# A graph network's layer-4 rows, made in another stage, and three blocks of small VectorE work in another

## The chip, the cores and the metric

The kernel runs on one core of one Trainium2 chip. The core has five engines that run side by side: TensorE (PE in the profile), VectorE (DVE), ScalarE (ACT), GpSimd (POOL) and SyncE (SP), and 16 DMA engines. They wait for each other through semaphores. The metric is the device time in microseconds: 2548.24 us before the change, the median of 3 runs (2527.15 to 2566.37).

## The reference, cut to what matters

Four graph layers on 50,000 nodes with 128 values each and 25,000 edges, sorted by destination. Each layer adds its result to `x` and normalizes the rows.

```python
x = _layernorm(x + _L0_gnn_ref(...))   # layer 1: two attention convolutions, 4 heads x 16, then 1 x 128
x = _layernorm(x + _L1_gnn_ref(...))   # layer 2: mean over the incoming edges
x = _layernorm(x + _L2_gnn_ref(...))   # layer 3: two-layer MLP per edge, then mean, max and sum
x = _layernorm(x + _L3_gnn_ref(...))   # layer 4: attention with both ends of the edge

def gat_layer(x, W, attn_l, attn_r, bias, src, dst, num_nodes):
    feat = (x @ W).reshape(num_nodes, H, D)
    e = jax.nn.leaky_relu(el[src] + er[dst], NEG_SLOPE)
    alpha = ee / s[dst]                                   # softmax over the edges of one destination
    return jax.ops.segment_sum(feat[src] * alpha[:, :, None], dst, num_segments=num_nodes) + bias
```

A node that is the destination of no edge (an isolated node) gets only biases and normalizations in every layer. Its row before layer 4 is therefore a scaled copy of its input row plus a combination of a few fixed bias rows, and the factors of that combination (the rates) follow from the mean, the variance and four dot products of the input row. An edge whose source is such a node needs this row in layer 4: these are the layer-4 rows of isolated sources. They are made for all edges, and a later index picks the ones that are wanted.

## The kernel before

The edges are handled in 49 groups (`NG`) of 512, as 4 tiles of 128 (`GT`). Every engine has its own program, and the whole is a sequence of stages with a barrier after each: a (gathers of the source and destination rows), b (the attention of layer 1's first convolution), c (the lookup stage), d (the projection of layer 1's second convolution), e, f, g and h for the other layers. In each stage the loops run over the 49 groups, and the order of each engine's program is the order of the code. There is no scheduler. `need(engine, name, n)` makes an engine wait until a semaphore has counted n groups; `S(name)` is that semaphore.

Stage b, about 597 to 757 us. For each group VectorE weighs the rows (L1129), TensorE turns them (L1211), VectorE sums over edges with a scan (L1148), ACT takes two Relus and an Exp (L1238 to L1242), VectorE joins them (L1199), TensorE multiplies (L1221), ACT copies to SBUF (L1250). `pipeline` runs these stages with lags and calls the blocks of its list `between` at evenly spaced steps. With two blocks they come at steps 24 and 48 of 51. VectorE's two are the first layer of the edge rates (`rates_vector`, L1064 to L1087) and `map_table`, which makes the table from which stage c looks up nodes. A layer of rates needs one square root from ACT (`rates_scalar`, L1103). Before `map_table` TensorE makes prefix sums (`prefix`, L1227).

Stage c, about 757 to 1045 us. The purpose is to find for each source the row of its first convolution, and to gather it. SP loads for each group the source numbers, copied to all partitions (`slb`, L1457), and the source rows from `xsrc_e` (L1460). VectorE compares the numbers (`hot`, L1345), TensorE looks up 4 tiles in `table` with eight matmuls (L1301, L1302), VectorE picks one value out of each row of the result (L1351), adds a bias to the source rows (`shifted`, L1368, into `z`), and writes four columns of indices (`hid`, L1358, L1361). GpSimd gathers with them four times 128 rows (L658). ACT normalizes the source rows (`apply`, L720), SP stores them (L1465), and ACT copies what was gathered one group before (`copy`, L1427, L1428). VectorE's order in group g is `hot(g+1)`, `pick(g)`, `shifted(g)`, `hid(g)`. SP's order is `load(g)`, `store(g-2)`. Between the groups VectorE has eight larger blocks (the table `extra`): after group 3 `rows_of_biases`, which makes the bias rows `DB`, after 5 and 7 the second and third layer of the edge rates, after 9, 11, 13, 15 and 16 the same for nodes. `QC` is 0, so the code for node rows in this stage (`node`, `rows`, `node_load`) does nothing.

Stage d, about 1067 to 1285 us. VectorE weighs and scans (L1133, L1148), TensorE turns (L1211) and multiplies (L1570), VectorE adds the residual and takes mean and variance (L1554, L674, L683), ACT normalizes (L720). Beside this the layer-4 rows are made: SP loads the source rows again (L1533), TensorE transposes the factors of the group (L1497), ACT copies them (L1516), TensorE adds the rows and the biases in PSUM (L1506 for the rows by the unit matrix, L1507 for factors times `DB`), ACT scales them in four ACTIVATEs (L1524), SP stores them (L1538).

## Time and profile before

| | us |
|---|---|
| median of 3 runs | 2548.24 |
| lowest and highest run | 2527.15, 2566.37 |
| profiled execution, its time | 2542.37 |
| its span, first to last instruction | 2540.6 |
| mean granted clock of TensorE | 0.679 of full speed |

The page of the profile gives busy time for each engine. Over the whole span TensorE is busy 1895.0 us (75%), VectorE 1740.2 (68%), GpSimd 1383.0 (54%), ScalarE 1083.8 (43%). These are sums over stages with different limits, so they must be read by stage. In the views, "idle before" is how long an engine stood before an instruction, and the arrow names what ended that. A granted clock of 1.0 is 2.4 GHz, one of 0.5 is 1.2 GHz. In a mean over a stretch anything between can stand.

### The profile page before, as it was taken

The numbers are of one execution on the slowest core, as the hardware profiler recorded it, in microseconds if no ns is written. First come the engines' busy times: TensorE is split into PE (matmuls) and PEld (weight loads), VectorE is DVE, ScalarE is ACT, GpSimd is POOL, SyncE is SP. The second block draws the span as 40 slices with busy tenths as digits, with TensorE's granted clock in tenths as the row PEclk, the third lists the DMA queues.
The fourth block names the chain that finished last, engine by engine and source line by source line (L and its number), as shares of the span: only waits on it lengthen the run. The fifth ranks groups of instructions, "written<-read, shape, count | busy, mean of one in ns | idle before, by whom it ended". The sixth has DMA issues, their size and how long they took to land.

```text
span 2540.6 us, 30997 instructions
## 1 busy us (share of the span) xinstructions
PE 1895.0 (75%) x7398; PEld 1202.8 (47%) x7398; DVE 1740.2 (68%) x6542; ACT 1083.8 (43%) x3008; POOL 1383.0 (54%) x1388
## 2 busy tenths in 40 slices
PE   3999999867874445399944454999998699959983
PEld 2898888855651112155534342444444122225542
DVE  6444445458769966598768885888887366678773
ACT  0222222215753343287633332666665455524332
POOL 4777777720006577200057771566666677727776
PEclk9656656655556665599756856999999555556565
DMA  4555555553334455288645554333332699933341
GB/s 154 160 155 157 155 152 160 159 188 133 125 127 125 112 156 160 72 278 262 211 131 155 154 159 120 98 112 111 109 106 82 237 363 326 313 105 100 122 135 37
DMA packets 255479, 398.63 MB, mean 157 GB/s; under 512 B 80999, under 2 KB 97536, under 8 KB 255172
## 3 DMA queue, kind: packets, MB, share of 16 engines
q1 hardware_dynamic: 204340, 307.86, 37.2%
q0 software_dynamic: 43904, 75.95, 11.0%
q10 hardware_dynamic: 7056, 12.85, 1.4%
q8 instruction: 62, 1.02, 0.2%
q14 instruction: 117, 0.96, 0.1%
HBM read 225.25 MB, written 178.97 MB: 159 GB/s over the span
## 4 chain that ended last, share of the span: by engine, by line
POOL 17%; issue 12%; PE 9%; DVE 9%; ACT 7%; DMA 3%; SPq 1%; POOLq 0%; DVEq 0%; ACTq 0%
POOL ring L658 9%; POOL big L658 4%; POOL out_dram L664 4%; ACT outr L720 3%; DVE big L1870 2%; ACT big L1809 2%; PE bank L1570 2%; DVE stats L674 2%; PE bank L1507 2%; PE bank L1506 2%; DMA ring<-x_t,idx 1%; PE bank L1211 1%; DVE z L1886 1%; DMA hT<-xsrc_e 1%; DVE mv L683 1%
## 5 line engine op out<-in xcount | busy, mean ns | idle before, releaser
L720 ACT ACTIVATE outr<-z,rn 128x128 f32<-128x128 f32 x784 | 322.7, 483 | 347.9 <-DVE rn L709 155.7
L658 POOL DMA_INDIRECT ring<-in_x_dram,idx x392 | 380.0, 969 | 147.3 <-issue 119.3
L658 POOL DMA_INDIRECT ring<-x_t,idx x280 | 269.0, 961 | 339.6 <-SPq L302 245.3
L658 POOL DMA_INDIRECT ring<-hidden_e,idx x196 | 193.3, 986 | 298.9 <-DVE idx L1361 241.6
L664 POOL DMA_INDIRECT x_t<-outr,idx x196 | 234.6, 1197 | 208.4 <-ACT outr L720 162.0
L1148 DVE TENSOR_TENSOR_SCAN G<-cont,G,bank 64x512 f32<-64x512 uint8 (+1 forms) x192 | 242.8, 1265 | 80.0 <-PE bank L1211 57.2
L664 POOL DMA_INDIRECT out_dram<-outr,idx x196 | 195.2, 996 | 102.7 <-issue 58.2
L1947 PE MATMUL bank<-DB,z 20*128 20x512 f32 x196 | 201.7, 1131 | 22.8 <-DVE xT L1337 7.0
L1020 DVE BATCH_NORM_STATS2 stats<-ring 128x6 f32<-128x128 f32 x196 | 42.8, 281 | 247.9 <-DMA ring<-in_x_dram,idx 247.9
L1301 PE MATMUL bank<-table,hT 128*128 128x391 bf16 x196 | 94.3, 481 | 153.4 <-DVE hT L1345 153.4
L674 DVE BATCH_NORM_STATS2 stats<-z 128x6 f32<-128x128 f32 x784 | 171.0, 281 | 5.1
L1211 PE MATMUL bank<-ident,msg 128*64 128x128 f32 (+1 forms) x588 | 136.3, 377 | 35.1 <-DVE msg L1133 32.2
L1570 PEld LDWEIGHTS bank<-W_s,G 65*128 65x128 f32 (+1 forms) x784 | 130.4, 252 | 65.4 <-issue 64.1
L1647 PE MATMUL bank<-ident,ring 128*128 128x128 f32 x196 | 47.8, 389 | 138.6 <-DMA ring<-x_t,idx 138.6
L1570 PE MATMUL bank<-W_s,G 65*128 65x128 f32 (+1 forms) x784 | 147.6, 348 | 0.0
L938 PEld LDWEIGHTS bank<-bT,msg 128*128 128x128 f32 x784 | 146.1, 277 | 1.0 <-ACT msg L977 0.9
L938 PE MATMUL bank<-bT,msg 128*128 128x4 f32 x784 | 143.5, 306 | 0.7 <-ACT msg L977 0.7
L977 ACT ACTIVATE msg<-bank 128x512 f32<-128x512 f32 x98 | 58.6, 598 | 188.8 <-PE bank L928 188.8
L1917 DVE CUSTOM_DVE_ANT_0 msg<-ring,attb 128x128 f32<-128x128 f32 x280 | 63.9, 288 | 101.9 <-DMA ring<-x_t,idx 59.3
L1211 PEld LDWEIGHTS bank<-ident,msg 128*64 128x64 f32 (+1 forms) x588 | 82.1, 163 | 93.1 <-issue 43.9
L658 POOL DMA_INDIRECT big<-x_t,idx x112 | 107.1, 956 | 34.2 <-issue 34.2
L716 ACT ACTIVATE sd<-mv,epsc 128x4 f32<-128x4 f32 x196 | 56.3, 287 | 157.8 <-DVE mv L683 157.8
(385 smaller groups left out, 4516.7 us busy)
## 6 DMA issues: line engine op xcount, KB each, us to landing
hT<-in_x_dram SPq DMA_DIRECT2D x194, 256.0 KB
ring<-x_e SPq DMA_DIRECT2D x147, 256.0 KB, 2.9
x_t<-outr SPq DMA_DIRECT2D x98, 256.0 KB, 2.7
x_e<-outr SPq DMA_DIRECT2D x98, 256.0 KB, 2.1
x_t<-xload SPq DMA_DIRECT2D x48, 512.0 KB, 3.1
xsrc_e<-ring SPq DMA_DIRECT2D x49, 256.0 KB, 2.1
xd_e<-ring ACTq DMA_DIRECT2D x49, 256.0 KB, 2.9
ring<-xsrc_e SPq DMA_DIRECT2D x49, 256.0 KB
```

The costliest lines, as they stand in the source:

```text
L658: nc.gpsimd.indirect_dma_start(to(c), None, table, bass.IndirectOffsetOnAxis(ap=idx[:, kind, (g + 1) * GT + c:(g + 1) * GT + c + 1].bitcas ...
L664: nc.gpsimd.indirect_dma_start(table, bass.IndirectOffsetOnAxis(ap=idx[:, kind, (g + 1) * GT + c:(g + 1) * GT + c + 1].bitcast(U32), axis= ...
L674: ins = v.bn_stats(stats[:, k, :], z[:, s, k, :])
L720: ins = nc.scalar.activation(to[:, k, :], frm[:, k, :], ACT.Identity, bias=sc[:, k, 1:2], scale=sc[:, k, 0:1])
L938: ins = nc.tensor.matmul(bank[4 + g % 2][:, at:at + 4], dxT[:, h, k * P:(k + 1) * P], bT[:], start=True, stop=True)
L977: nc.scalar.activation(dxT[:, q % 2, :], bank[0][:], ACT.Copy).then_inc(S("n_dxT"), 1)
L1148: return v.tensor_tensor_scan(o, m, src_ap, ini, ALU.mult, ALU.add)
L1211: ins = nc.tensor.transpose(bank[s][0:width, c * P:(c + 1) * P], msg[:, s, c, 0:width], ident[:])
L1301: nc.tensor.matmul(o, lhs, table[:, 0, :], start=True, stop=False)
L1570: ins = nc.tensor.matmul(bank[2 + s][:, c * F:(c + 1) * F], G[0:k, s, c * P:(c + 1) * P], W[:], start=not b, stop=not b or c == GT - 1)
L1917: c.do(v.tensor_tensor_reduce(msg[:, n, k, :], frm, attb[:, n, :], 1.0, 0.0, ALU.mult, ALU.add, dots[:, k, n:n + 1]))
L1947: nc.tensor.matmul(bank[2 + q % 4][:], ecT[q % 4], DB[0:GT * CN, :, :].rearrange("p t f -> p (t f)"), start=True, stop=True).then_inc(S("o ...
```

## The change

The layer-4 rows of isolated sources are made in stage c and no longer in stage d. They use the source rows that stage c has in SBUF anyway (`rload`), so the second load from `xsrc_e` is gone. The matmuls, the ACTIVATEs and the store are the same. In stage c TensorE has them after the lookups of the next group, ACT between the copy of the gathers and the normalization, SP after the store of the layer-1 rows. The lookups use five PSUM banks and no longer six.

For this the rates of all edges must be there before stage c. So the second and third layer of the edge rates and `rows_of_biases` go to stage b, whose list has now five blocks, at steps 12, 20, 28, 36 and 48: first layer, `map_table`, second layer, `rows_of_biases`, third layer. The code for node rows in stage c, which did nothing, is gone too.

```diff
@@ -1190,6 +1190,20 @@
                 c.hold()
             return step
 
+        def rows_of_biases(v):
+            ch = Chain(v)
+
+            def step():
+                for t in range(GT):
+                    for k, n in ((0, 1), (1, 2), (2, 3), (3, None), (4, 0)):
+                        row = ones[0:32, :] if n is None else biasc[0:32, n, :]
+                        at = ident[0:32, CN * t + k:CN * t + k + 1]
+                        if k == 0:
+                            ch.link(v.tensor_scalar(DB[:, t, :], row, at, None, ALU.mult))
+                        else:
+                            ch.link(v.scalar_tensor_tensor(DB[:, t, :], row, at, DB[:, t, :], ALU.mult, ALU.add))
+            return step
...
+            edge = rates_vector(v, 3, "e", ecov, est, alpha3, est, etemps)
             pipeline(v, [(-1, weighing(v, "b", feat, HF, HEADS)), (2, join), (0, scanning(v, "b", HF))],
-                     [rates_vector(v, 3, "e", ecov, est, alpha3, est, etemps)[0], map_table(v)])
+                     [edge[0], map_table(v), edge[1], rows_of_biases(v), edge[2]])
...
-            pipeline(pe, [(0, turning(pe, "b", HF)), (2, project)], [skip, prefix])
+            pipeline(pe, [(0, turning(pe, "b", HF)), (2, project)], [prefix, skip, skip, skip, skip])
...
+            root = rates_scalar(a, 3, "e", etemps)
+            pipeline(a, [(0, split), (2, rows)], [root[0], skip, root[1], skip, root[2]])
...
+        sx = xTf[:, 0:2 * GE].rearrange("p (s e) -> p s e", s=2)
+
+        def local_tensor(pe):
+            def factors(g):
+                need(pe, "s_ecT", g)
+                nc.tensor.transpose(bank[6][0:GT * CN, 0:P], ecov[:, four(g), :].rearrange("p t k -> p (t k)"),
+                                    ident[:]).then_inc(S("s_tr"), 1)
+
+            def local(g):
+                s = g % 2
+                wait(pe, f"c_ld{g % RING}", 16 * (g // RING + 1))
+                need(pe, "s_ecT", g + 1)
+                need(pe, "s_row", g - 1)
+                nc.tensor.matmul(bank[5 + 2 * s][:], ident[:], rload[:, g % RING].rearrange("p t f -> p (t f)"), start=True, stop=False)
+                nc.tensor.matmul(bank[5 + 2 * s][:], hcT[g % 4], DB[0:GT * CN, :, :].rearrange("p t f -> p (t f)"),
+                                 start=False, stop=True).then_inc(S("s_mm"), 1)
+            return factors, local
+        def local_scalar(a):
+            def factors(g):
+                need(a, "s_tr", g + 1)
+                need(a, "s_mm", g - 3)
+                nc.scalar.activation(hcT[g % 4], bank[6][0:GT * CN, 0:P], ACT.Copy).then_inc(S("s_ecT"), 1)
+
+            def local(g):
+                need(a, "s_mm", g + 1)
+                if g >= 2:
+                    wait(a, f"s_out{g % 2}", 16 * (g // 2))
+                for k in range(GT):
+                    ins = nc.scalar.activation(sx[:, g % 2, k * F:(k + 1) * F], bank[5 + 2 * (g % 2)][:, k * F:(k + 1) * F],
+                                               ACT.Copy, scale=alpha3[:, GT * g + k:GT * g + k + 1])
+                ins.then_inc(S("s_row"), 1)
+            return factors, local
+
+        def local_store(sp, g):
+            need(sp, "s_row", g + 1)
+            sp.dma_start(edge_row(x3s_e, g), sx[:, g % 2, :]).then_inc(S(f"s_out{g % 2}"), 16)
...
-                    need(pe, "look_pick", t - 5)
-                    o = bank[t % 6][:, 0:HI]
+                    need(pe, "look_pick", t - 4)
+                    o = bank[t % 5][:, 0:HI]
...
+            factors, local = local_tensor(pe)
             for g in range(NG):
                 look(g)
+                factors(g)
+                if g:
+                    local(g - 1)
+            local(NG - 1)
...
-            edge = rates_vector(v, 3, "e", ecov, est, alpha3, est, etemps)
...
-            extra = {3: rows_of_biases, 5: edge[1], 7: edge[2], 9: node[0], 11: node[1], 13: node[2], 15: node[3],
-                     16: scaled}
+            extra = {9: node[0], 11: node[1], 13: node[2], 15: node[3], 16: scaled}
...
-            root = rates_scalar(a, 3, "e", etemps)
...
+            factors, local = local_scalar(a)
             for g in range(NG + 1):
                 if g in extra:
                     extra[g]()
                 if g < NG:
+                    factors(g)
+                if g:
+                    local(g - 1)
+                if g < NG:
                     apply(g)
...
                 need(sp, "c_z", g - 3)
+                need(sp, "s_mm", g - 3)
                 sp.dma_start(rload[:, g % RING].rearrange("p t f -> p (t f)"), edge_row(xsrc_e, g)) \
                     .then_inc(S(f"c_ld{g % RING}"), 16)
...
                 if g >= 2:
                     store(g - 2)
...
+                    local_store(sp, g - 2)
...
-            if tag == "d":
-                factors, local = local_tensor(pe)
-                pipeline(pe, [(0, turning(pe, tag, width)), (0, factors), (1, project), (1, local)])
-            else:
-                pipeline(pe, [(0, turning(pe, tag, width)), (1, project)])
+            pipeline(pe, [(0, turning(pe, tag, width)), (1, project)])
...
-            linear_sync(sp, "d", xd_e, x1_e, False, "_z", also=local_sync(sp))
-            for s in range(2):
-                sp.wait_ge(S(f"s_out{s}"), 16 * len(range(s, NG, 2)))
+            linear_sync(sp, "d", xd_e, x1_e, False, "_z")
```

What this does to the order of instructions is seen at three places. The first is SP's program at the start of stage c, before the change. `hT<-srclo_d` are the source numbers, `ring<-xsrc_e` the source rows, `x_t<-outr` the store of the layer-1 rows.

```order
L1457 DMA hT<-srclo_d 128x512
L1460 DMA ring<-xsrc_e 128x512
L1465 DMA x_t<-outr 128x512 [waits g_row]
L1457 DMA hT<-srclo_d 128x512 [waits look_oh]
L1460 DMA ring<-xsrc_e 128x512 [waits g_z]
```

The same place with the change. `x_t<-xT` is the store of the layer-4 rows.

```order
L1475 DMA hT<-srclo_d 128x512
L1479 DMA ring<-xsrc_e 128x512
L1484 DMA x_t<-outr 128x512 [waits g_row]
L1345 DMA x_t<-xT 128x512 [waits s_row]
L1475 DMA hT<-srclo_d 128x512 [waits look_oh]
L1479 DMA ring<-xsrc_e 128x512 [waits s_mm,g_z]
```

Before each load of source numbers there stands now a store that waits for `s_row`, which ACT counts up after the four ACTIVATEs of the layer-4 rows.

The second place is ACT's program in stage c, one group, before the change: `big<-ring` is the copy of the gathers, `outr<-z,est` the normalization.

```order
L1427 ACTIVATE big<-ring 128x4x64 [waits g_in0]
L1428 ACTIVATE big<-ring 128x4
L720 ACTIVATE outr<-z,est 128x128 [waits g_out2,g_z]
L720 ACTIVATE outr<-z,est 128x128 x3
L1427 ACTIVATE big<-ring 128x4x64 [waits g_in1]
```

And with the change. `g_in` is the landing of the gathers.

```order
L1451 ACTIVATE big<-ring 128x4x64 [waits g_in1]
L1452 ACTIVATE big<-ring 128x4
L1331 ACTIVATE hT<-bank 20x128 [waits s_mm,s_tr]
L1338 ACTIVATE xT<-bank,dlo 128x128 [waits s_out0,s_mm]
L1338 ACTIVATE xT<-bank,dlo 128x128 x3
L720 ACTIVATE outr<-z,est 128x128 [waits g_out3,g_z]
L720 ACTIVATE outr<-z,est 128x128 x3
```

The factors (L1331) and the layer-4 rows (L1338) stand now directly behind the copy of the gathers, and before the next normalization.

The third place is VectorE's program in stage b with the change, around step 28. The block of the second layer (L1064 to L1089) stands between a scan (L1148) and the next weighing (L1129); before the change no block stood there.

```order
L1213 SCALAR_TENSOR_TENSOR hT<-hT 64x512 [waits b_exp,g_mm]
L1148 SCALAR_TENSOR_TENSOR G<-cont,G,bank 64x512 [waits b_exp,g_scan,g_tr]
L1064 SCALAR_TENSOR_TENSOR cv<-ecov,cv 128x196
L1065 TENSOR_SCALAR cv<-cv,BB 128x196 [waits dve_chain]
L1067 RECIPROCAL cv<-cv 128x196 [waits e_root]
L1069 SCALAR_TENSOR_TENSOR ecov<-ecov,BB,cv 128x196 [waits dve_chain]
L1072 TENSOR_TENSOR cv<-cv 128x196
L1073 TENSOR_TENSOR cv<-cv 128x196 [waits dve_chain]
L1083 TENSOR_TENSOR dlo<-dlo,cv 128x196
L1089 TENSOR_TENSOR ecov<-ecov,cv 128x196 [waits dve_chain]
L1129 TENSOR_TENSOR msg<-big,alpha 128x4x64 [waits g_tr,dve_chain]
```

On ACT the square roots of these layers (`e_root`) come with a load of the activation table before them, and another before the next Exp: there are six table loads in stage b now, and there were two.

## Rows read from the trace of the kernel before

**Rows 1.** Stretches b, c, d: PE, PEld, DVE, ACT, POOL busy; clock, DMA share, GB/s

```profile
597.00:757.00 160.00, 140.73 (x577) 112.14 (x576) 113.93 (x167) 106.65 (x242) 0.00 (x0) 0.51 0.32 123
757.00:1045.00 288.00, 121.53 (x392) 46.78 (x392) 212.40 (x658) 106.09 (x301) 193.28 (x196) 0.62 0.49 135
1067.00:1285.00 218.00, 206.52 (x833) 110.90 (x833) 177.24 (x638) 148.39 (x491) 0.00 (x0) 0.85 0.75 237
```

**Rows 2.** Groups by line, stage c: GpSimd's gathers, busy, mean ns, idle before

```profile
L658 POOL DMA_INDIRECT ring<-hidden_e,idx x196 | 193.3, 986 | 298.9 <-DVE idx L1361 241.6 <-issue 55.2 <-ACT big L1428 2.1
```

**Rows 3.** Timeline, stage c: start us, length us, engine, line, idle before

```profile
949.17 1.46 POOL L658 DMA_INDIRECT ring<-hidden_e,idx  x1 [0.30 <-issue]
...
954.69 0.94 POOL L658 DMA_INDIRECT ring<-hidden_e,idx  x1 [0.30 <-issue]
...
958.23 0.42 ACT L1427 ACTIVATE big<-ring 128x256 f32<-128x256 f32 x1 [5.85 <-DMA ring<-hidden_e,idx]
...
960.67 0.43 SPq L1457 DMA_DIRECT2D hT<-srclo_d  x1
...
960.91 0.42 ACT L1427 ACTIVATE big<-ring 128x256 f32<-128x256 f32 x1 [0.62 <-DMA ring<-hidden_e,idx]
...
963.35 0.57 SPq L1457 DMA_DIRECT2D hT<-srclo_d  x1
...
964.29 0.35 DVE L1345 TENSOR_SCALAR hT<-hT,pcol 128x512 bf16<-128x512 bf16 x1 [3.40 <-DMA hT<-srclo_d]
...
967.58 0.16 DVE L1361 SCALAR_TENSOR_TENSOR idx<-hidt,dhi 128x4 int32<-128x4 f32 x1
...
967.91 0.43 DVE L1345 TENSOR_SCALAR hT<-hT,pcol 128x512 bf16<-128x512 bf16 x1 [0.16 <-DMA hT<-srclo_d]
```

**Rows 4.** Timeline, stage d: first at 2.4 GHz, then TensorE at 1.2 GHz

```profile
1132.54 1.09 ACT L1524 ACTIVATE xT<-bank,dlo 128x128 f32<-128x128 f32 x4
...
1132.76 1.27 DVE L1148 TENSOR_TENSOR_SCAN G<-cont,G,bank 64x512 f32<-64x512 uint8 x1
...
1136.52 1.27 DVE L1148 TENSOR_TENSOR_SCAN G<-cont,G,bank 64x512 f32<-64x512 uint8 x1
...
1224.35 1.92 PE L1506 MATMUL bank<-hT,ident 128*128 128x512 f32 x2
1226.19 2.07 PE L1507 MATMUL bank<-DB,hT 20*128 20x512 f32 x2
```

**Rows 5.** Timeline, stage b, around the first layer of the edge rates, engine by engine

```profile
658.09 0.47 DVE L1064 SCALAR_TENSOR_TENSOR cv<-ecov,est 128x196 f32<-128x196 f32 x1
...
662.18 1.38 DVE L1067 RECIPROCAL cv<-cv 128x196 f32<-128x196 f32 x1 [3.27 <-ACT cv L1103]
...
666.75 0.43 DVE L1129 TENSOR_TENSOR msg<-big,alpha 128x256 f32<-128x256 f32 x1
...
660.40 1.28 ACT L1103 ACT_TABLE_LOAD   x1
661.69 0.46 ACT L1103 ACTIVATE cv<-cv,epsc 128x196 f32<-128x196 f32 x1
...
667.83 1.97 PE L1221 MATMUL bank<-W2x,hT 64*128 64x66 f32 x8 [8.09 <-DVE hT L1199]
```

**Rows 6.** Timeline, end of stage b: from the first instruction of `map_table`

```profile
739.29 0.56 DVE L1173 COPY xT<-bank 128x391 f32<-128x391 f32 x1 [3.53 <-PE bank L1228]
...
746.58 0.68 DVE L1199 SCALAR_TENSOR_TENSOR hT<-hT 64x512 f32<-64x512 f32 x1
```

**Rows 7.** Stretches of stage c, VectorE: `DB`, edge layers 2, 3, node rates

```profile
777.60:785.07 7.47, 6.77 (x21) 0.74 0.57 168
791.83:796.72 4.89, 4.19 (x9) 0.80 0.59 154
803.48:807.14 3.66, 2.78 (x7) 0.71 0.47 125
814.47:872.75 58.28, 54.41 (x119) 0.62 0.39 103
```

110 lines of the change are left out of this document (5 added, 105 removed).

## The prediction

> **What bounds the kernel now.** I read the view by stretches first, to see which engine fills each of the three stages that the change touches [rows 1]. In the layer-1 attention (597 to 757 us) TensorE is busy 140.7 of 160 us and VectorE 113.9. In the lookup stage (757 to 1045) nobody is full by busy time: VectorE 212.4 of 288, GpSimd 193.3, TensorE 121.5 at a mean granted clock of 0.62. In the layer-1 projection (1067 to 1285) TensorE is busy 206.5 of 218.
>
> Then the groups by line. GpSimd's 196 gathers take 986 ns each, and each is followed by some 0.3 us of "issue" (55.2 us in 181 cases) [rows 2]: 1.25 us apiece, 5.0 us a group of four, 49 groups = 246 us. So GpSimd paces the lookup stage; its waits for VectorE's indices are 241.6 us, of which one of 217 is the time before the stage, so 24 us inside it. 9 us of start, 241 us to the last group (48 x 5.02), 24 of waits, and some 8 for the last gathers and copies make 282 of the 286 seen.
>
> Then the timeline, for two neighbouring groups of the same stage, to see how far GpSimd is from being held up. The gathers of one group start at 949.17 (124 stand before that one) and ACT copies them at 958.23; the next start at 954.69 and are copied at 960.91: 9.1 and 6.2 us. SP issues the load of the source numbers (`slb`) at 960.67; VectorE gets it at 964.29, 3.6 us later, and has written the next indices at 967.58 + 0.16, 3.45 us after that. The next load takes from 963.35 to 967.91, 4.6 us [rows 3].
>
> In the projection stage the scans of VectorE stand 3.76 us apart when the clock is 2.4 GHz (1132.76, 1136.52) [rows 4], which is VectorE's own work of a group. When TensorE has 1.2 GHz, the two 512-column matmuls of the layer-4 rows take 1.84 us from one to the next, then 2.07 [rows 4], TensorE is the bound and a group takes more.
>
> **The change, part by part.**
>
> *1. The projection stage loses the layer-4 rows*: 49 times a transpose, two 512-column matmuls, five ACTIVATEs, a 256 KB load and a 256 KB store. What is left for TensorE lies under VectorE's 3.76 us at either clock: the transposes and the projection are what now takes turns with 3.9 us of row matmuls (1.84 + 2.07). So VectorE paces the stage: 48 x 3.76 = 180.5 us from the first scan, plus about 2 ahead and 10 for the last group's chain = 193, against 218: **-25 us**. Bounds: -20 (a third of the groups slow for another reason) and -31 (the 41 us in which VectorE is idle now [rows 1], less those 10).
>
> *2. The layer-1 attention gets three blocks of VectorE work*: the two later layers of the edge rates and the 20 small operations that make `DB`. In the lookup stage they took 4.89, 3.66 and 7.47 us from end to end, VectorE busy for 4.19, 2.78 and 6.77 [rows 7]. The rate layers need a root from ACT, and here ACT also runs Exp. The one layer that stands here already shows the price: ACT first finishes its group, loads a table (1.28 us) and takes the root, so that VectorE stands 3.27 us; VectorE is away from 658.09 to 666.75, 8.66 us, and TensorE idles 8.09 [rows 5]. TensorE is the bound here, so what VectorE loses beyond 0.6 us is lost. The new ones: 4.19 + 3.27 = 7.5, less 0.6 = 6.9; `DB` 7.5 - 0.6 = 6.9. The table of nodes (`map_table`) moves from the end to the middle. At the end it costs a wait of 3.53 us for TensorE's prefix sums and then runs until 746.58, from 739.29: 10.8 in all [rows 6]. In the middle it costs 7.3 - 0.6 = 6.7, and the prefix matmuls are free: they fall into the gap at the first layer. At the end stands the third layer instead, 2.78 + 3.27 = 6.1 us, plus 1.28 for the table that the last Exp needs again, 7.4: 3.4 less than now. Sum: 6.9 + 6.9 + 6.7 - 3.4 = **+17 us**. Bounds: +8 (half of each stall caught up, as VectorE has 46 us idle in the stage [rows 1]) and +23.
>
> By the Trainium skill, ScalarE: Activation LUTs, section "What ACT_TABLE_LOAD costs", a switch of tables is 1283 ns plus a drain of 1380 ns, 2.66 us in all. The trace agrees with the first and not with the second: load at 660.40, the root starts at 661.69 [rows 5]. By the page's price the four new switches would add 4 x 1.38 = 5.5 us at most, and this part would be +23 and not +17.
>
> *3. The lookup stage loses those three blocks*: by length they are 16 of the 50 us of such blocks in the stage, so 8 of GpSimd's 24 us of waits would be theirs, less since they come while VectorE is still ahead: **-5 us**, between 0 and -8. What stays are the five blocks of the node rates, 58.28 us [rows 7] with seven groups of 3.45 inside, so 34 us.
>
> *4. The lookup stage gets the layer-4 rows.* By work nobody is full. ACT: 106.1 us now [rows 1], 2.2 a group, plus 1.3. TensorE: its 392 matmuls take 121.5 us at clock 0.62 [rows 1], 0.31 each, 2.5 us a group, about 2.6 at 1.2 GHz; the added matmuls are 3.9 at 1.2 GHz [rows 4] and half at 2.4, with 0.2 for a transpose: 6.7 or 3.4 us. DMA share 0.49 now; half of what the projection stage moves goes.
>
> But the order makes a **new ring of waits**. SP's order is: source numbers, source rows, store of layer-1 rows, then the new store of layer-4 rows, and only then the next source numbers. The new store of group g waits for ACT's rows of g, and these stand on ACT behind the copy of the gathers of g-1. The next load on SP is that of the numbers of g+3, which VectorE needs before it writes the indices of g+2. So with the change the gathers of n hold up those of n+3. Before it they hold up only those of n+4, because ACT normalizes group g before it copies g-1, and SP waits for that alone. Once round, from rows: gathers to copy 9.1 or 6.2, mean 7.6 [rows 3]; copy, factors and rows on ACT 0.4 + 0.2 + 1.1 (the four ACTIVATEs are 1.09 [rows 4]); store issued, 0.4; numbers to VectorE 3.6 or 4.6, mean 4.1 [rows 3]; to the indices 3.45 [rows 3]; GpSimd starts its next DMA 0.3 later. 17.6 us for three groups: 5.9 a group. With the short landings 5.2, with 9.1 and a landing of 4.6 it is 6.5. The same sum for four groups today is about 18 / 4 = 4.5, below 5.02: that is why GpSimd paces the stage now. Other rings lie just below (ACT's apply, copy, rows, SP, numbers, VectorE's `z`: 10.8 for two groups, 5.4), and TensorE's own 6.7 counts whenever it has 1.2 GHz; so I take 6.1.
>
> The stage: 9 of start, 48 x 6.1 = 293, the five node blocks, which stand two groups apart and so meet 2 x (6.1 - 3.45) = 5.3 us of slack between one and the next, leave 34 - 4 x 5.3 = 13; 7.5 at the end. 322 against 286: **+36 us**, the -5 of part 3 included, since the node blocks alone are counted. Bounds: 5.9 gives +28, 6.3 gives +44.
>
> **Sum**: 17 + 36 - 25 = +28 us on the profiled execution's 2542.4: 2570. The median of the runs is 2548.24, 6 us above, and they spread from 2527 to 2566. Against the median the same +28 would be 2576; I keep the 2570 of the profiled execution, which is nearer the middle of the three. About 2% (51 us) is what a measurement of this kernel tells from no change; this forecast is inside it.
>
> **Rivals.**
>
> *GpSimd still paces the lookup stage* (the other side: not slower). If the landings stay at the short end (6.2 and 3.6 us), the ring is 15.7 / 3 = 5.2, next to 5.02, and the stage is GpSimd's as now: -5, and 48 x 0.1 = 5 for what the ring still lacks. For it: the landing of a gather alternates, and is 6.2 in every second group. Against: a store more stands in front of the loads. Decides at 5.02 x 3 = 15.1 us round. Sum: 17 + 0 - 25 = -8, with part 2 at its low end -17: 2530 to 2540. Chance 0.2.
>
> *TensorE becomes the bound of the lookup stage at 1.2 GHz*: 48 x 6.7 = 322, + 9 + 6 + 7.5 = 344: +58, and in all +50: 2592 to 2605. For it: the stage has 0.62 now, and the attention stage has 0.51 with TensorE busy 88% [rows 1]. Against: the projection stage, which holds these same matmuls, has 0.85 [rows 1]. The Trainium skill, TensorE: Matmul & The Clock Gate, Part 1, says that the throttled state is the default and activity releases it; by that the added matmuls lift the clock, TensorE needs 3.4 us, and this rival falls away. The 0.51 of the attention stage speaks against taking busy time for activity, so I leave it a chance: 0.16.
>
> *The blocks moved to the attention are mostly covered there*: part 2 is +8 and the rest as forecast: +17, 2560. It lies in my own range, chance within it.
>
> **How the numbers follow.** Forecast (ring of about 6 us, attention +17, projection -25): 0.6, own range 2553 to 2582 (parts at their bounds). GpSimd's pace 0.2. TensorE at 1.2 GHz 0.16. 0.04 for something unseen, such as landings that grow with the added store (a ring of 7 us is +75 in the stage, 2610). Range 2532 to 2602: it leaves out the lower part of the first rival and the upper one of the second. Faster by over 2% (under 2497): even -25, -5 and nothing for part 2 is -30, so 0.03. Slower by over 2% (above 2599): half of the second rival and the unseen, 0.12. Within: 0.85.
>
> **What the changed profile would show.** Lookup stage: gathers about 6 us a group, GpSimd idle "<-DVE idx" in most groups, VectorE idle "<-DMA" of the source numbers in front of `oht`, SP waiting for the layer-4 rows on ACT and no longer for the layer-1 rows. If GpSimd has groups of 5.0 us and no such waits, part 4 is wrong. If TensorE is busy above 95% there at clock 0.5, the second rival is right. Attention: four gaps of TensorE of about 7 us in place of one, and a shorter one at the end. Projection: scans 3.76 us apart throughout, stage near 193 us, whatever the clock. A stage longer than 205 would break part 1.

## The result and the profile after

| | before | after |
|---|---|---|
| median, us (4 runs each) | 2537.69 | 2558.72 |
| lowest and highest, us | 2520.94, 2566.37 | 2556.19, 2562.63 |
| profiled execution, its time | 2542.37 | 2556.19 |
| its span | 2540.6 | 2554.5 |
| mean granted clock | 0.679 | 0.664 |

The ratio of after to before is 1.0122, with a 95% interval of 1.007 to 1.0175. The kernel is a little slower, by less than the 2% that counts as a difference here. The forecast was 2570 in a range of 2532 to 2602, "within 2%" at 0.85. By the medians the difference is +21.0 us, by the profiled pair +13.9.

Cut into stages, the two profiled executions differ like this. A stage is measured from the first instruction that belongs to it alone: for b the first weighing, for c the first load of source numbers, up to the last copy of gathers, for d the first weighing, up to the first gather of stage e.

| us | before | after | difference | forecast |
|---|---|---|---|---|
| up to stage b | 590.6 | 585.2 | -5.4 | 0 |
| b, attention | 166.0 | 183.5 | +17.5 | +17 |
| c, lookup | 286.2 | 325.4 | +39.2 | +36 |
| between c and d | 24.9 | 24.9 | 0 | 0 |
| d, projection | 218.3 | 183.2 | -35.1 | -25 |
| the rest | 1254.6 | 1252.3 | -2.3 | 0 |
| span | 2540.6 | 2554.5 | +13.9 | +28 |

The view by stretches of the kernel after answers to [rows 1]. The columns are start and end, length, PE, PEld, DVE, ACT, POOL busy, then the clock, the DMA share and GB/s. The three lines are stages b, c and d.

```profile
597.00:775.00 178.00, 138.03 (x563) 109.14 (x563) 125.55 (x201) 108.41 (x240) 0.00 (x0) 0.51 0.30 113
775.00:1097.00 322.00, 239.46 (x631) 79.10 (x628) 198.37 (x619) 165.80 (x544) 189.18 (x196) 0.75 0.53 157
1117.00:1330.00 213.00, 147.14 (x641) 125.28 (x640) 187.79 (x690) 100.47 (x257) 21.06 (x23) 0.51 0.42 137
```

In stage c TensorE's work has doubled, from 121.5 us to 239.5, and yet it is busy for only 74% of the stretch. ACT is busy for half of it. GpSimd has the same work as before and stands more. Nothing is full, so the stage must be paced by waits. (The third stretch is longer than stage d: it takes in the start of stage e.)

**Stage c.** The groups by line of the kernel after, GpSimd in stage c: busy time, mean ns, then the idle time before them. It answers to [rows 2].

```profile
L658 POOL DMA_INDIRECT ring<-hidden_e,idx x196 | 189.2, 965 | 359.6 <-DVE idx L1402 311.2 <-issue 48.4
```

The waits of the kernel after, stages b's end and c: who waited, for whom, us in total, times, longest.

```profile
POOL ring L658 <- DVE idx L1402: 311.2, 38, 234.6
DVE hT L1386 <- DMA hT<-srclo_d: 117.0, 42, 8.9
...
ACT outr L720 <- DVE z L1409: 81.0, 41, 5.8
...
ACT big L1451 <- DMA ring<-hidden_e,idx: 37.7, 20, 4.1
```

GpSimd's longest wait, 234.6 us, is the time before the stage. The other 37 make 76.6 us, where before it was 24.2 (241.6 - 217.4 [rows 2]). From the start of the first gather to the end of the last the sum is 189.2 busy + 48.4 issue + 76.6 of waits = 314 us, which is what the trace measures; before, it was 193.3 + 55.2 + 24.2 + 2.1 = 275, also as measured. So the gathers and what goes with them took 13 us less, and the waits for VectorE's indices 52 us more: the loss of the stage, 39, lies in these waits. VectorE in turn waited 42 times, 117.0 us, for the source numbers to land. So the next question is when SP issued their load. SP's own waits in the kernel after, over the same stretch:

```profile
SPq L1345 <- ACT xT L1338: 136.4, 48, 7.0
SPq L1484 <- ACT outr L720: 103.4, 48, 6.9
```

Before, the store of the layer-1 rows was nearly all that SP waited for there (213.8 us in 49 waits). Now the new store of the layer-4 rows (L1345) waits in every group but one, and the load of the numbers stands behind it. The timeline of the kernel after, ten microseconds of steady work: start, length, engine, line, and in brackets the idle time before.

```profile
993.58 0.42 ACT L1451 ACTIVATE big<-ring 128x256 f32<-128x256 f32 x1 [2.59 <-DMA ring<-hidden_e,idx]
...
994.15 1.09 ACT L1338 ACTIVATE xT<-bank,dlo 128x128 f32<-128x128 f32 x4
...
995.03 0.69 DVE L1409 TENSOR_TENSOR z<-ring,biasc 128x512 f32<-128x512 f32 x1
...
995.27 0.32 SPq L1345 DMA_DIRECT2D x_t<-xT  x1
...
995.64 0.43 SPq L1475 DMA_DIRECT2D hT<-srclo_d  x1
995.75 1.65 ACT L720 ACTIVATE outr<-z,est 128x128 f32<-128x128 f32 x4 [0.51 <-DVE z L1409]
...
997.87 1.09 ACT L1338 ACTIVATE xT<-bank,dlo 128x128 f32<-128x128 f32 x4
...
998.99 0.32 SPq L1345 DMA_DIRECT2D x_t<-xT  x1
999.35 0.43 SPq L1475 DMA_DIRECT2D hT<-srclo_d  x1
...
999.90 0.35 DVE L1386 TENSOR_SCALAR hT<-hT,pcol 128x512 bf16<-128x512 bf16 x1 [3.85 <-DMA hT<-srclo_d]
```

This is the ring that the prediction described, link by link. ACT had waited 2.59 us for a gather, copied it at 993.58, and (behind the factors, 0.25 us) made the layer-4 rows at 994.15. The store followed at 995.27 and the numbers at 995.64, and VectorE had them at 999.90, after 3.85 us without work. The second turn in the same rows is the other ring named there: VectorE's `z` (995.03), ACT's normalization (995.75), the rows (997.87), the store (998.99), the numbers (999.35). In between ACT copied the next gathers without waiting. Over the calm part, 940 to 1060 us, the stretch view counts 78 gathers in 120 us, which is 6.15 us a group; the forecast was 6.1, with 5.02 before. The links have the lengths that were put in: VectorE has the numbers 3.4 to 4.9 us after their issue where it waited for them, median 4.1 (forecast 4.1), and ACT has a group's gathers 6.8 to 9.4 us after their first start where it waited, median 8.2 (forecast 7.6).

**Stage b.** The timeline of the kernel after, TensorE in stage b: all lines with 5 us or more of idle time before them, and the prefix sums ahead of the first.

```profile
618.61 1.67 PE L1242 MATMUL bank<-xT,DB 128*128 128x391 f32 x2
620.08 1.51 PE L1243 MATMUL bank<-xT,ones 128*128 128x391 f32 x2
...
627.77 1.97 PE L1236 MATMUL bank<-W2x,hT 64*128 64x66 f32 x8 [5.33 <-DVE hT L1213]
...
657.67 1.97 PE L1236 MATMUL bank<-W2x,hT 64*128 64x66 f32 x8 [6.68 <-DVE hT L1213]
...
687.91 1.97 PE L1236 MATMUL bank<-W2x,hT 64*128 64x66 f32 x8 [7.02 <-DVE hT L1213]
...
717.75 1.97 PE L1236 MATMUL bank<-W2x,hT 64*128 64x66 f32 x8 [6.62 <-DVE hT L1213]
...
758.00 3.75 PE L1236 MATMUL bank<-W2x,hT 64*128 64x66 f32 x16 [5.46 <-DVE hT L1213]
```

These are the five blocks, 30 us apart or so: first layer, `map_table`, second layer, `DB`, third layer. Together 31.1 us. Before, there were two such gaps, 8.09 and 7.22, together 15.3. The difference, 15.8, is nearly the whole of the +17.5. The first gap is shorter than the 8.09 of before because the prefix matmuls now run in it: they hold TensorE for 2.77 us (618.61 to 621.38), and 5.33 + 2.77 = 8.10. VectorE is away as long as before, 618.02 to 626.70.

**Stage d.** The timeline of the kernel after, VectorE's scans:

```profile
1148.99 1.24 DVE L1148 TENSOR_TENSOR_SCAN G<-cont,G,bank 64x512 f32<-64x512 uint8 x1
...
1152.52 1.24 DVE L1148 TENSOR_TENSOR_SCAN G<-cont,G,bank 64x512 f32<-64x512 uint8 x1
...
1156.05 1.24 DVE L1148 TENSOR_TENSOR_SCAN G<-cont,G,bank 64x512 f32<-64x512 uint8 x1
```

They stand 3.53 us apart (every eighth time or so 3.73, the mean of 48 is 3.56), not 3.76, and that at a granted clock of 0.50, TensorE's lower level of 1.2 GHz. The stretch from 1120 to 1280 us shows who paces it:

```profile
1120.00:1280.00 160.00, 123.65 (x538) 105.20 (x537) 153.88 (x567) 84.59 (x216) 0.00 (x0) 0.50 0.44 145
```

VectorE is busy for 153.9 of 160 us, 3.42 in each of 45 groups, and TensorE for 77%. The chain that ended last says the same, 1140 to 1165 us (its share of the time, by line):

```profile
by line: DVE G L1148 32.3%; DVE stats L674 24.8%; DVE z L1512 19.9%; DVE mv L683 9.8%; issue 6.4%; DVE rn L700 4.7%; DVE msg L1133 2.8%; DVE rn L692 1.9%
```

### The profile page after: what moved, and what is told of

Read it like the earlier page. It is cut to its first block, busy times and chain, and to the rows that moved or that the text cites. A ratio compares the mean times of both kernels' runs of the same rounds, so it can differ in the third digit from the quotient of the medians.

```text
span 2554.5 us, 31000 instructions
## 1 busy us (share of the span) xinstructions
PE 1945.6 (76%) x7398; PEld 1239.8 (49%) x7398; DVE 1737.4 (68%) x6542; ACT 1097.6 (43%) x3012; POOL 1376.2 (54%) x1388
## 3 DMA queue, kind: packets, MB, share of 16 engines
q1 hardware_dynamic: 197284, 295.01, 35.1%
## 4 chain that ended last, share of the span: by engine, by line
POOL 18%; DVE 14%; issue 13%; ACT 6%; DMA 2%; PE 2%; POOLq 1%; SPq 0%; DVEq 0%; ACTq 0%
POOL ring L658 9%; POOL out_dram L664 5%; POOL big L658 4%; DVE stats L674 3%; ACT outr L720 3%; DVE big L1820 2%; DVE G L1148 2%; ACT big L1759 2%; DVE mv L683 1%; DVE z L1512 1%; DVE z L1836 1%; DMA ring<-x_t,idx 1%; SPq L1659 0%; DVE msg L1867 0%; POOLq L302 0%
## 5 line engine op out<-in xcount | busy, mean ns | idle before, releaser
L658 POOL DMA_INDIRECT ring<-hidden_e,idx x196 | 189.2, 965 | 359.6 <-DVE idx L1402 311.2
L1148 DVE TENSOR_TENSOR_SCAN G<-cont,G,bank 64x512 f32<-64x512 uint8 (+1 forms) x192 | 241.5, 1258 | 52.4 <-PE bank L1226 32.4
L1226 PE MATMUL bank<-ident,msg 128*64 128x128 f32 (+1 forms) x588 | 154.9, 418 | 66.0 <-DVE msg L1133 63.1
L1528 PEld LDWEIGHTS bank<-W_s,G 65*128 65x128 f32 (+1 forms) x784 | 167.8, 315 | 68.0 <-issue 65.5
L1528 PE MATMUL bank<-W_s,G 65*128 65x128 f32 (+1 forms) x784 | 185.5, 413 | 0.4 <-DVE G L1148 0.4
L1355 PE MATMUL bank<-table,hT 128*128 128x391 bf16 x196 | 85.5, 436 | 73.0 <-DVE hT L1386 71.4
L1226 PEld LDWEIGHTS bank<-ident,msg 128*64 128x64 f32 (+1 forms) x588 | 90.6, 178 | 99.3 <-DVE msg L1133 77.3
```

What stands on the lines that cost most here:

```text
L658: nc.gpsimd.indirect_dma_start(to(c), None, table, bass.IndirectOffsetOnAxis(ap=idx[:, kind, (g + 1) * GT + c:(g + 1) * GT + c + 1].bitcas ...
L1148: return v.tensor_tensor_scan(o, m, src_ap, ini, ALU.mult, ALU.add)
L1226: ins = nc.tensor.transpose(bank[s][0:width, c * P:(c + 1) * P], msg[:, s, c, 0:width], ident[:])
L1355: nc.tensor.matmul(o, lhs, table[:, 0, :], start=True, stop=False)
L1528: ins = nc.tensor.matmul(bank[2 + s][:, c * F:(c + 1) * F], G[0:k, s, c * P:(c + 1) * P], W[:], start=not b, stop=not b or c == GT - 1)
```

## The experiments

There are twelve runs on three chips, of eight kernels (the two of the change among them). Times and lengths of stages are compared only on one chip, each kernel with the runs of the kernel before there. The four of the second chip came first, then those of the first chip, then those of the third. On the first of them the kernel before has a median of 2536.9 us (13 runs, 2517.95 to 2565.13), as in the first measurement. On the two others it has 2923.03 (25 runs) and 2928.91 (31 runs): they are about 15% slower, for the kernel before and for all others. What that did to the experiments is told with them.

### On the first chip: both kernels again, the store later, and a version

**c_before and c_after** are the two kernels unchanged.

> The kernel before, profiled on the chip of the next three kernels, so that stages are compared on one chip. Attention stage 166 us, lookup stage 286, projection stage 218, if the chip is like that of the first profiles.

> The changed kernel again, for the same reason: attention 183 us, lookup 325, projection 183, in all 1.2% slower than before.

c_before took 2521.62 us in its one run. c_after: 2561.56, ratio 1.0105 (1.005 to 1.016).

**e5_later_again** is the kernel after with one store in another place. SP stores the layer-4 rows of group g after the load of g+3 and not of g+2.

```diff
-            for g in range(NG + 2):
+            for g in range(NG + 3):
                 if g < NG:
                     load(g)
-                if g >= 2:
+                if 2 <= g < NG + 2:
                     store(g - 2)
-                    local_store(sp, g - 2)
+                if g >= 3:
+                    local_store(sp, g - 3)
```

> The store of the layer-4 rows one group later on SP, again, beside the changed kernel on one chip. Ring theory: GpSimd paces the lookup stage at 5.0 to 5.2 us a group, the stage takes 282 to 295 us, 30 to 40 less than the changed kernel, and SP waits less than 10 us for the layer-4 rows. Rival, the added work slows it: within 8 us of the changed kernel.

Measured: 2519.02 us, ratio to before 0.995 (0.9921 to 0.9979). Stages, with the same kernels on the same chip:

| us | up to b | b | c | c to d | d | rest | span |
|---|---|---|---|---|---|---|---|
| c_before | 589.1 | 166.0 | 284.2 | 24.9 | 199.9 | 1255.8 | 2519.9 |
| c_after | 589.8 | 183.5 | 328.2 | 24.1 | 183.1 | 1254.2 | 2562.9 |
| e5_later_again | 585.3 | 183.4 | 282.8 | 24.8 | 183.1 | 1252.9 | 2512.3 |
| e6_version | 590.4 | 167.7 | 280.8 | 24.9 | 183.1 | 1256.7 | 2503.6 |

One store in another place takes 45.4 us from stage c, and nothing else moves beyond 5 us. The medians of the two kernels, 4 and 10 runs, lie 42.5 us apart. The layer-4 rows are still made there, with the same matmuls, ACTIVATEs and DMAs. SP's waits show that the place of the store is what it was. First c_after, end of stage b and stage c, then e5_later_again, the same:

```profile
SPq L1345 <- ACT xT L1338: 140.2, 49, 9.5
SPq L1484 <- ACT outr L720: 101.4, 47, 6.9
```

```profile
SPq L1484 <- ACT outr L720: 184.7, 49, 7.9
...
SPq L1345 <- ACT xT L1338: 2.0, 1, 2.0
```

And the waits of the engines, c_after:

```profile
POOL ring L658 <- DVE idx L1402: 312.3, 36, 234.5
DVE hT L1386 <- DMA hT<-srclo_d: 119.1, 41, 8.8
```

and e5_later_again:

```profile
POOL ring L658 <- DVE idx L1402: 252.6, 5, 234.6
ACT big L1451 <- DMA ring<-hidden_e,idx: 74.2, 41, 4.1
DVE hT L1386 <- DMA hT<-srclo_d: 72.7, 40, 8.8
```

Of GpSimd's 35 short waits 4 are left, 77.8 us of them have become 18.0. VectorE still waits for the numbers in 40 groups, but for less, and it no longer matters: a wait that is not on the path remains in the list. Now ACT waits for the gathers (41 times), so GpSimd paces the stage. The stretch view, GpSimd's gathers between 900 and 1000 us of either, c_after:

```profile
900.00:1000.00 100.00, 63.73 (x68) 0.82 0.62 176
```

and e5_later_again:

```profile
900.00:1000.00 100.00, 76.27 (x78) 0.88 0.70 203
```

68 gathers are 5.9 us a group, 78 are 5.1. The clock is 0.88 here and 0.82 there, which raises the question whether the store or the clock did it. In stage c neither GpSimd nor VectorE waits for TensorE in either kernel. But ACT does: for the matmuls of the layer-4 rows 22.1 us in 17 waits in c_after, and 2.2 in 3 in e5_later_again, so TensorE is at times a link of the ring. The order of SP is what was edited, and a higher clock comes with more work done in the time. Two runs on the other chips settle it: there the pace is that of the open ring at the clock of the kernel after (see the end of the third chip).

**e6_version** joins what the other kernels pointed to. On top of e5_later_again the numbers of a group are loaded one group ahead of its rows, `DB` gets memory of its own and is made in stage a after its group 8 (there VectorE waits for gathers), and each layer of rates is cut in two, so that VectorE asks for the root in one block (`ask`), does the work of other groups, and takes it in the next (`rest`).

```diff
+                if g == 8:
+                    biases()
...
-                     [edge[0], map_table(v), edge[1], rows_of_biases(v), edge[2]])
+                     [edge[0][0], edge[0][1], map_table(v), edge[1][0], edge[1][1], edge[2][0], edge[2][1]] + [skip] * 4)
...
-            pipeline(a, [(0, split), (2, rows)], [root[0], skip, root[1], skip, root[2]])
+            pipeline(a, [(0, split), (2, rows)], [root[0], skip, skip, root[1], skip, root[2]] + [skip] * 5)
...
             def load(g):
+                if g + 1 < NG:
+                    numbers(g + 1)
```

> The later store, and also: the source numbers loaded one group further ahead, the bias rows made by VectorE in the first stage (half idle there), and each layer of the edge rates split in two, so that its root is asked for four groups before it is used. Theory: lookup 282 to 290 us. Attention: the three waits of 3.3 us for roots and the 7 us of the bias rows go, and nothing stands in the tail: 183 - 10 - 7 = 166. In all 35 + 17 = 50 us below the changed kernel and 25 to 35 below the kernel before, 1.2% faster than it. Rival for the attention: a stall there costs by what TensorE and ACT have to restart and not by VectorE's length, then it stays above 178.

Measured: 2500.34 us, ratio to before 0.9858 (0.9803 to 0.9914). It is the fastest kernel here and beats both of the change, clear of noise, though by less than 2% over the kernel before. Stage b has 167.7 us, as before the change, though it holds the two layers more. In TensorE's timeline only two gaps of over 3 us are left inside it, 3.97 and 6.67. Of its four parts the later store was run alone on this chip, and the numbers ahead on another; the other two only together.

### On the second chip

**e1_store_later** is the kernel e5_later_again.

> SP issues the store of the layer-4 rows one group later, behind the store of the layer-1 rows of the next group; all work stays. Ring theory: the gathers of n then hold up those of n+4, the round is about 19 us for four groups, 4.9, and GpSimd paces the lookup stage again at 5.0 to 5.2 us a group: the stage loses 30 to 40 of its 325 us, GpSimd's waits for indices inside it fall from 77 us to under 40, total about 2520. Rival, the added work itself (TensorE, ACT or the added 256 KB store) slows the stage: it stays within 8 us of 325.

**e2_blocks_only** is the kernel before with the three blocks moved to stage b and nothing else; the layer-4 rows stay in stage d.

```diff
-                     [rates_vector(v, 3, "e", ecov, est, alpha3, est, etemps)[0], map_table(v)])
+                     [edge[0], map_table(v), edge[1], rows_of_biases(v), edge[2]])
...
-            extra = {3: rows_of_biases, 5: edge[1], 7: edge[2], 9: node[0], 11: node[1], 13: node[2], 15: node[3],
+            extra = {9: node[0], 11: node[1], 13: node[2], 15: node[3],
```

> The kernel before with only the three VectorE blocks moved from the lookup stage to the attention stage, in the same order as in the changed kernel; the layer-4 rows stay in the projection stage. Theory: the attention stage takes 17 us more (183 for 166), the lookup stage 5 less, the projection stage is unchanged at 218: 12 us slower in all. Rival, the blocks are covered by VectorE's idle time in the attention stage: at most 8 more there, in all no change.

**e3_no_bias_matmul** is the kernel after without the second of the two 512-column matmuls, so its layer-4 rows lack the bias part.

```diff
-                nc.tensor.matmul(bank[5 + 2 * s][:], ident[:], rload[:, g % RING].rearrange("p t f -> p (t f)"), start=True, stop=False)
-                nc.tensor.matmul(bank[5 + 2 * s][:], hcT[g % 4], DB[0:GT * CN, :, :].rearrange("p t f -> p (t f)"),
-                                 start=False, stop=True).then_inc(S("s_mm"), 1)
+                nc.tensor.matmul(bank[5 + 2 * s][:], ident[:], rload[:, g % RING].rearrange("p t f -> p (t f)"), start=True,
+                                 stop=True).then_inc(S("s_mm"), 1)
```

> The changed kernel without the second matmul of the layer-4 rows (factors times bias rows), so these rows lack their bias part. TensorE loses 49 x 1.05 to 2.0 us of the lookup stage. Ring theory: TensorE is not the bound, but the matmul stands in the ring that goes numbers, lookup, rows, ACT, SP; that ring is the shorter one, so the stage loses 0 to 12 us. Rival, TensorE is the bound whenever its clock is low: the stage loses 30 us or more.

**e4_copy_lag2**: ACT copies the gathers two groups late and not one, so that it does not wait for them ahead of the layer-4 rows.

```diff
-            for g in range(NG + 1):
+            for g in range(NG + 2):
...
-                if g:
+                if 0 < g <= NG:
                     local(g - 1)
...
-                if g:
-                    copy(g - 1)
+                if g >= 2:
+                    copy(g - 2)
```

> The changed kernel with ACT's copy of the gathers one group later, so that the layer-4 rows of n+2 (not n+1) stand behind the copy of n. The ring through the gathers gets a fourth group (17.6 / 4 = 4.4 us); the ring through z, the normalization, the rows, SP and the numbers (11.4 us for two groups, 5.7) stays. If the gathers' ring alone holds the stage, it loses 35 us or more; if the two lie close together, as the rows say, the stage goes from 6.0 to about 5.7 us a group and loses 10 to 20; if the gathers' ring has no part, it loses nothing.

| | median, us | ratio to before | c | d | up to b |
|---|---|---|---|---|---|
| before | 2923.03 | | | | |
| e1_store_later | 2928.8 | 1.0028 (0.9993 to 1.0062) | 330.1 | 183.2 | 788.0 |
| e2_blocks_only | 2962.88 | 1.016 (1.0095 to 1.0226) | 306.4 | 223.1 | 798.5 |
| e3_no_bias_matmul | 2920.72 | 1.001 (0.9972 to 1.0047) | 323.6 | 183.3 | 778.0 |
| e4_copy_lag2 | 2927.56 | 1.0028 (0.9996 to 1.0061) | 331.8 | 183.3 | 790.5 |

Stage b has 183.4 to 183.9 us in all four, and stage d the length it has elsewhere, so stage b can be read, and d where its clock does not change. In e2_blocks_only b is 183.5 as well. With the layer-4 rows still in d, that shows the +17.5 to be the price of the blocks alone. Its sum was missed: +12 us was expected, and 1.016 is +47 (28 to 66). Stage d has 223.1 us for the 218 expected, with ten of its steps at 6.62 us. The rest can't be placed, as the kernel before has no profile on this chip.

Stage c can't be read by its length. The kernel e1_store_later is the one that has 282.8 us on the first chip, and here it has 330.1, where 285 to 295 was expected. The timeline of e1_store_later, all engines, one moment of stage c:

```profile
1112.71 0.62 DVE L1392 SCALAR_TENSOR_TENSOR msg<-iota,shi,bank 128x391 bf16<-128x391 f16 x1 [4.27 <-remote]
...
1113.47 0.27 ACT L1331 ACTIVATE hT<-bank 20x128 f32<-20x128 f32 x1 [5.49 <-remote]
...
1115.28 0.94 POOL L658 DMA_INDIRECT ring<-hidden_e,idx  x1 [4.42 <-DVE idx L1402]
```

VectorE stands 4.27 us in the middle of a group, before the third of four equal instructions, and the profile names no local cause ("remote"). Its waits over 990 to 1300 us:

```profile
DVE msg L1392 <- remote: 39.3, 10, 8.5
...
ACT hT L1331 <- remote: 32.2, 9, 5.5
...
ACT xT L1338 <- remote: 21.8, 5, 8.0
```

In stage c the kernel after has no such line in the first measurement. GpSimd's waits that follow stand about 25 us apart (1115.28, 1141.37, 1166.47, 1192.65; 4.4 to 6.0 us each). All sixteen short waits of GpSimd in the stage are 69.5 us; without them its gathers would take 248 us from first to last and not 318. A kernel whose ring takes 6 us a group loses part of the same time to these stalls, and the two costs don't add up. Since the kernel after itself did not run on this chip, times and lengths tell nothing on the ring. The steps from one group to the next do, and they stand at the end of the next section.

### On the third chip

Three of them were repeated, and one part of the version was run alone. This chip stalls like the second.

**e7_numbers_ahead** is the kernel after with the numbers loaded one group ahead, its stores as they were.

```diff
-            def load(g):
+            def numbers(g):
                 need(sp, "look_oh", g - 3)
...
+            def load(g):
+                if g + 1 < NG:
+                    numbers(g + 1)
...
+            numbers(0)
```

> The changed kernel with the source numbers loaded one group further ahead on SP; both stores stay where the change has them. Ring theory: SP still waits for the layer-4 rows, but the numbers that come behind that wait are needed one group later, so each ring gets one group more (gathers 4, z 3) and the lookup stage goes to GpSimd's pace: 283 to 292 us for 328. Rival, it was the place of the store itself (its DMA next to the others) that cost: it stays above 315.

**e8_copy_lag2, e9_no_bias_matmul, e10_blocks_only** are e4, e3 and e2 again.

> ACT's copy of the gathers one group later, again. Two rings of nearly one length (gathers 5.9 us a group, z 5.7): the lookup stage goes from 328 to 310 to 318. If the gathers' ring alone holds the stage, below 300; if it has no part, 328.

> Without the second matmul of the layer-4 rows, again; the rows lack their bias part. If TensorE's work counts only inside the rings: 0 to 12 us less than 328 in the lookup stage. If TensorE bounds the stage when its clock is low: 30 or more.

> The kernel before with only the three blocks moved, again: attention 183.5 for 166, lookup 280 for 285, projection as before (200 to 218): 12 us slower in all than the kernel before.

| | median, us | ratio to before | c | d | up to b |
|---|---|---|---|---|---|
| before | 2928.91 | | | | |
| e7_numbers_ahead | 2924.99 | 1.0004 (0.9975 to 1.0033) | 330.8 | 183.3 | 787.7 |
| e8_copy_lag2 | 2931.76 | 1.0021 (0.9984 to 1.0058) | 336.6 | 183.3 | 783.2 |
| e9_no_bias_matmul | 2922.05 | 0.9976 (0.9947 to 1.0006) | 329.2 | 183.3 | 777.5 |
| e10_blocks_only | 2945.89 | 1.0068 (1.0032 to 1.0104) | 308.0 | 229.2 | 789.0 |

By length none of the four kernels does what was expected in c (e9_no_bias_matmul misses by 1 us): 283 to 292 for e7_numbers_ahead, 310 to 318 for e8_copy_lag2, up to 12 us less than 328 for e9_no_bias_matmul, 280 for e10_blocks_only. e10_blocks_only repeats b at 183.5 us. With +20 us (9 to 30) for the 12 expected, it and e2_blocks_only are the only kernels here that are slower than the kernel before by more than their interval: they pay for the blocks in b and keep d at 223 to 229 us.

What can be read on the two chips is the step from one group to the next, since a stall hits one group in four or five. The table takes the starts of each group's first gather (GpSimd's timeline) and, behind the node blocks, the 31 steps from group 18 to group 49.

| | chip | median step, us | steps over 5.6 us, of 31 |
|---|---|---|---|
| before, c_before | first measurement, first | 5.00, 5.00 | 0, 0 |
| after, c_after | first measurement, first | 5.90, 5.99 | 22, 22 |
| e5_later_again, e6_version | first | 5.01, 5.00 | 0, 0 |
| e2_blocks_only, e10_blocks_only | second, third | 5.03, 5.15 | 7, 8 |
| e1_store_later | second | 5.19 | 9 |
| e7_numbers_ahead | third | 5.15 | 10 |
| e4_copy_lag2, e8_copy_lag2 | second, third | 5.73, 5.68 | 16, 16 |
| e3_no_bias_matmul, e9_no_bias_matmul | second, third | 5.94, 5.82 | 19, 19 |

Each row rests on one trace per kernel, and the kernel after stands in it from another chip than e1 to e4 and e7 to e9. But kernels without the ring have 5.0 to 5.2 on all three chips, so the rows can be laid side by side.

*e7_numbers_ahead* keeps both stores where the change has them, and SP waits for the layer-4 rows nearly as long (136 and 140 us in the two traces of the kernel after). SP's waits, the end of b and stage c:

```profile
SPq L1345 <- ACT xT L1338: 129.2, 27, 12.6
SPq L1488 <- ACT outr L720: 32.7, 25, 6.4
```

Yet its steps are 5.15. So the store's place costs next to nothing by itself: what costs is that the numbers needed next stand behind its wait. By length, 330.8, the rival ("above 315") would have looked right; the 330.8 are steps of 5 us with one of 7 to 11 in every fourth or so, where the engines stall.

*e4_copy_lag2 and e8_copy_lag2* open the ring through the gathers alone: ACT waits for gathers once and twice in the stage, where it was 20 times. The step stays at 5.7 (at a clock of 0.72 in e4_copy_lag2), as expected, which is then the other ring, the one through `z`. *e3_no_bias_matmul and e9_no_bias_matmul* take a matmul of 1.05 to 2 us from TensorE in each group, and the step loses 0 to 0.2 us. Over 48 steps that is at most 8 us, within the 0 to 12 expected. A stage bounded by TensorE was to lose 30, or 0.6 a step.

The clock is not the cause of the slower step. The stretch view over these groups, all engines, the kernel after and then e7_numbers_ahead:

```profile
898.00:1087.00 189.00, 150.99 (x395) 49.13 (x394) 107.52 (x374) 103.31 (x343) 118.14 (x125) 0.77 0.57 170
```

```profile
1099.00:1295.00 196.00, 143.98 (x393) 49.70 (x392) 108.43 (x371) 99.55 (x339) 118.87 (x124) 0.76 0.55 162
```

At 0.77 the closed ring has steps of 5.90, at 0.76 the open one has 5.15; e1_store_later has 0.76 as well.

One comparison within the second chip goes against the first chip. Stage c has 330.1 us in e1_store_later, with the layer-4 rows and an open ring, and 306.4 in e2_blocks_only, without the rows. The steps between the stalls are nearly the same, but those that a stall hits have 8.6 to 10.8 us and 7.6 to 9.4. There the added work costs 24 us even with the store moved. Why a stall costs more beside it was not looked for.

## Why the prediction was right, point by point

**Stage b, +17: right, by its own steps.** Measured +17.5, and in all eleven traces of kernels with the five blocks the stage has 183.4 to 183.9 us. Forecast were four gaps of about 7 us and a shorter one at the end. Three are 6.6 to 7.0 (6.7, 6.9 and 6.9 by the sum) and the last is 5.46. The first has 5.33 of idle time and 2.77 of prefix matmuls, together the 8.09 of before [rows 5], so that "the prefix matmuls are free: they fall into the gap at the first layer" came out to the letter. The measured +17.5 agrees with 1.28 us for a load of the table and nothing more. The price of 2.66 us for each switch, by the Trainium skill (ScalarE: Activation LUTs, section "What ACT_TABLE_LOAD costs"), would have made the part +23 by the prediction's estimate, and that is not seen.

**Stage c, +36: right, and its mechanism was tested.** Measured +39.2 in the first pair and +44.0 in the pair on the first chip, against bounds of +28 to +44. The ring was forecast at 6.1 us a group, and the calm part has 6.15 (5.9 in c_after). Every sign named for it is in the trace: GpSimd waits for indices in most groups, VectorE for the source numbers, SP for the layer-4 rows. The proof is e5_later_again. It breaks the ring and keeps the work, and the stage falls from 328.2 to 282.8 us, below the 284.2 of before. That stage of before still held the three blocks. They cost it 5.1 us, as forecast (-5): behind them GpSimd waits for indices 2.8, 1.7 and 0.6 us (at 788.8, 800.5 and 810.9 in the kernel before, and the same in c_before), and these waits are gone in e5_later_again. So on this chip the layer-4 rows themselves cost the stage some 4 us (one trace each; the two of the kernel after differ by 3), and 45 of the loss was the load that stood behind one waiting store. Of the two rings that meet in that store, one through the gathers (5.9 by the sum) and one through `z` (5.4), the rows show both: 37.7 us of ACT's waits for gathers and 81.0 for `z`. Moving the store opens both. e4_copy_lag2 and e8_copy_lag2 open the first alone, and the step goes from 5.9 or 6.0 to 5.7 and not to 5.0. So the two are nearly of one length, the one through `z` takes about 5.7 by itself and not 5.4, and only a change that opens both gives the 45 us. One reading in the sum was high: 9.1 us from gathers to copy [rows 3] is among the longest of the steady groups before (6.1 to 9.2, in turn short and long), but with the change the mean is 7.8, so the 7.6 that was used holds.

**Stage d, -25: the mechanism was right, the term was mis-sized.** It measured -35.1 in the first pair. Two errors lie in it. (A step is here the time from one scan of VectorE to the next.) The first is in "3.76 us apart when the clock is 2.4 GHz [rows 4], which is VectorE's own work of a group". It was not. The stretch view of the kernel before, 1100 to 1220 us:

```profile
1100.00:1220.00 120.00, 116.17 (x515) 62.46 (x515) 110.18 (x403) 92.20 (x309) 0.00 (x0) 0.96 0.86 271
```

In 31 groups VectorE was busy for 110.2 us, 3.55 a group, and TensorE for 116.2, 3.75 a group and 97% of the time. The chain that ended last, 1110 to 1150 us, where the granted clock is 1.00, runs through TensorE alone:

```profile
by line: PE bank L1506 29.9%; PE bank L1507 27.8%; PE bank L1570 24.6%; PE bank L1211 15.4%; PE bank L1497 3.0%; issue 0.8%
```

So even at the high clock it was TensorE that the stage waited for. Without its layer-4 work the mean step is 3.56: 48 x (3.76 - 3.56) = 10 us, which is the miss of 10. It would have been seen ahead by dividing busy time by groups: VectorE's 177.2 us [rows 1] over 49 are 3.6. The second is that "218 us" is not a property of the kernel before. In c_before the same stage has 199.9 us, at a mean granted clock of 0.94 from 1067 to 1267 where the first trace has 0.88 (0.85 over its whole stage [rows 1]). In both, a step has 3.6 to 3.9 us at the high clock and 6.62 at the low one (14.00 us of TensorE in the 14 from 1258 to 1272, at 0.50). The first trace holds more of the long ones, and its 48 steps are 201.1 us where c_before has 184.8: 16.3 of the 18.4 us between the two stages. Against that pair the term is -16.8. In both the kernel after has 183 us at about 0.5: by taking the matmuls away the change makes the stage independent of the clock, as forecast. It fits with this that the four runs of the kernel after lie within 6.4 us and the four of before within 45; that the clock in this stage is all of the spread was not shown.

**The sum.** +28 was forecast, +13.9 is the difference of the profiled pair: -10 from stage d, -5.4 from the time up to stage b and -2.3 from the rest, which the change does not touch, +3.7 from b and c. In the second pair it is +43.0: 17.5 + 44.0 - 16.8 and -1.7 from elsewhere. The forecast lies between the two; that it lies so near the middle is luck. In the first pair stage d and the stages that the change leaves alone gave 18 us more than forecast, in the second d gave 8 us less and c cost 8 more. The prediction's own range of 2553 to 2582 is called "parts at their bounds", but the bounds add up to +5 to +47, 2547 to 2589. The choice of the profiled execution as a base (stage d at its long end) is worth more than any error in b and c.

**The rivals.** *GpSimd still paces the lookup stage* fell: the landings did not stay at the short end of 6.2 and 3.6 us, the medians are 8.2 and 4.1 where they were waited for. e5_later_again, where GpSimd does pace the stage, shows its price: 0.995 of 2536.9, which is -13, and -7.6 by the profiled pair, for the -8 forecast. That is near, but stage by stage it is +17.4, -1.4 and -16.8 against c_before, where the rival had 17, 0 and -25. *TensorE becomes the bound at 1.2 GHz* fell by its own test: it is busy 74% of stage c at 0.75, not above 95% at 0.5, and taking a matmul away gave at most 0.2 us a group (e3, e9). Its sum has a slip: by its own step of 6.7 the node blocks would add 8 and not 6. The row agrees with the rule that stood beside it (Trainium skill, TensorE: Matmul & The Clock Gate, Part 1: activity releases the clock) as far as the stage goes, 0.62 before and 0.75 after, with twice the work. Stage b speaks against reading the rule as busy time: 138.0 of 178 us busy after the change and 140.7 of 160 before, and 0.51 in both. *The blocks are mostly covered in the attention* fell: +8 forecast, +17.5 measured.
